# Decay matrices and v as float16 halves, v transposed by DMA, the state's fading on GpSimd, and a new order of steps on every engine

## What is computed

```python
z, x, B_proj, C_proj, dt_logits = split(u @ in_proj_w)
x = silu(causal_conv1d(x, conv_weight, conv_bias))        # 4 taps; gives v, 16 heads x 64
k, q = elu(B_proj) + 1, elu(C_proj) + 1                   # 64 states, shared by the heads
a = exp(-softplus(dt_logits + dt_bias) * exp(A_log))      # decay of each head and token
# inside a chunk: y_intra = ((q k^T) * exp(cs_s - cs_t), lower triangle) v
# between chunks: y_inter = exp(cs) q h_prev;  h = d * h + (k scaled)^T v
y = y_intra + y_inter + D_param * v
y = y * rsqrt(mean(y * y) + eps) * norm_scale * silu(z)
return y @ out_proj_w
```

## Time and profile before

| | |
|---|---|
| median of 3 runs | 1983.89 us (1983.5 to 1985.98) |
| profiled execution | 1986.14 us, its span 1984.4 us |
| mean granted TensorE clock | 0.973 of full speed |
| PE busy | 1877.7 us, 95% |
| DVE busy | 1470.5 us, 74% |
| ACT busy | 1019.4 us, 51% |
| POOL busy | 182.4 us, 9% |
| DMA | 107.37 MB, main queue 18.3% of 16 engines |

### The profile page before, as it was taken

One profiled execution on the slowest core, in us unless ns is written; L12 is line 12 of the kernel. 1 busy time (PEld: TensorE's weight loads), 2 busy tenths in 40 slices (PEclk: granted clock), 3 DMA queues, 4 the chain that ended last, 5 costly groups with the idle time before them and its releaser, 6 DMA issues.

```text
span 1984.4 us, 39342 instructions
## 1 busy us (share of the span) xinstructions
PE 1877.7 (95%) x13426; PEld 1337.4 (67%) x13426; DVE 1470.5 (74%) x3279; ACT 1019.4 (51%) x2247; POOL 182.4 (9%) x150
## 2 busy tenths in 40 slices
PE   5446899999999999999999999999999999999999
PEld 2123777767686767767676877777676867777675
DVE  6897686867677686867677686868677786867676
ACT  7836544536364554546363644546363645445363
POOL 0430010101000010101000010101000000101010
PEclk9668899999999999999999999999999999999999
DMA  8101112121212111121212111121212111121212
GB/s 321 68 19 35 28 44 64 37 54 53 54 43 49 47 43 48 37 54 53 54 46 49 43 45 46 37 58 49 53 54 43 53 40 40 40 67 37 53 54 53
DMA packets 147857, 107.37 MB, mean 54 GB/s; under 512 B 110030, under 2 KB 111158, under 8 KB 147254
## 3 DMA queue, kind: packets, MB, share of 16 engines
q1 hardware_dynamic: 147238, 105.51, 18.3%
q10 hardware_dynamic: 528, 1.05, 0.2%
HBM read 72.18 MB, written 8.65 MB: 41 GB/s over the span
## 4 chain that ended last, share of the span: by engine, by line
PE 92%; DVE 4%; ACT 1%; DVEq 1%; DMA 1%; issue 1%; SPq 0%; ACTq 0%; PEldq 0%
PE bank L827 88%; DVE wi L587 2%; PE bank L648 1%; PE bank L894 1%; PE bank L639 1%; DVEq L523 0%; DMA wi<-n_L_attn_out_proj_w_dram 0%; DVE wug L547 0%; DVE big L437 0%; PE bank L621 0%; DVE wd L437 0%; ACT wi L363 0%; DVE su_scale L526 0%; ACT wi L393 0%; ACT big L389 0%
## 5 line engine op out<-in xcount | busy, mean ns | idle before, releaser
L827 PE MATMUL bank<-xnT,wug 128*128 128x256 f16 x6144 | 705.1, 273 | 0.0
L827 PEld LDWEIGHTS bank<-xnT,wug 128*128 128x128 f16 x6144 | 600.6, 98 | 99.9
L827 PE MATMUL bank<-wd,h 128*128 128x512 f16 x1536 | 371.0, 379 | 0.0
L827 PEld LDWEIGHTS bank<-wd,h 128*128 128x128 f16 x1536 | 148.4, 100 | 157.2 <-issue 3.4
L1079 POOL TENSOR_TENSOR vw<-v,dec 128x512 f32<-128x512 f32 x64 | 73.9, 1155 | 1689.7 <-ACT v L1029 1239.7
L827 PE MATMUL bank<-wi,xnT 128*128 128x512 f16 (+1 forms) x1152 | 204.2, 330 | 16.4 <-DMA xnT<-cvx 16.4
L986 ACT ACTIVATE tg<-bank,gate_scale 128x256 f32<-128x256 f32 x256 | 119.7, 467 | 174.7 <-PE bank L827 139.1
L1035 ACT ACTIVATE Mx<-Mx,cs_own 128x128 f32<-128x128 f32 x512 | 162.1, 389 | 50.0 <-DMA Mx<-cs_rows 50.0
L1163 DVE SCALAR_TENSOR_TENSOR cvx<-xc,conv,cvx 128x256 f32<-128x256 f32 x384 | 169.0, 481 | 14.5
L827 PE MATMUL bank<-xnT,wi 128*128 128x256 f16 x1536 | 172.9, 273 | 0.0
L827 PEld LDWEIGHTS bank<-wi,xnT 128*128 128x128 f16 x1152 | 101.4, 99 | 104.6 <-issue 17.2
(11 more groups left out here) (241 smaller groups left out, 2386.5 us busy)
## 6 DMA issues: line engine op xcount, KB each, us to landing
Mx<-cs_rows SPq DMA_DIRECT2D x128, 256.0 KB, 3.5
cvx<-in_L_attn_u_dram SPq DMA_DIRECT2D x17, 512.0 KB, 3.4
Mx<-in_L_attn_u_dram SPq DMA_DIRECT2D x16, 512.0 KB, 3.7
out_dram<-Mx SPq DMA_DIRECT2D x16, 512.0 KB, 2.8
big<-in_L_ffn_W_down_dram SPq DMA_DIRECT2D x2, 2048.0 KB, 12.2
wug<-in_L_attn_in_proj_w_dram SPq DMA_DIRECT2D x2, 2048.0 KB, 12.8
pair<-in_L_ffn_W_gate_dram SPq DMA_DIRECT2D x4, 1024.0 KB, 5.3
pair<-in_L_ffn_W_up_dram SPq DMA_DIRECT2D x3, 1024.0 KB, 5.5
```

What stands on the lines that cost most here:

```text
L827: ins = nc.tensor.matmul(out, lhsT, rhs, start=first and n == 0, stop=last and n == len(pairs) - 1)
```

## The change

1. itr takes float16 halves. DVE's dec result M is followed by two new steps: mh (ACT copies M to float16, `M_hi`) and ml (DVE subtracts, `M_lo`). The halves lie in the bytes of M itself, or one q further. A scale C_M is folded into G, and itr's result is scaled back on DVE by S_ITR.
2. v is split into halves before it is turned: th on ACT (`v_hi`), tl on DVE (`v_lo`), and td on SP transposes both by DMA into the new array `v16`, tokens on partitions. The vt steps of PE and ACT go. itr is 8 heads x three products of float16, 64 columns each.
3. POOL first adds the two halves of v (into `vd`), then multiplies as before; its scales are folded elsewhere. y is written over v16 as float32.
4. sd: the state's multiplication by its decay goes from DVE to POOL, with a new semaphore `state_faded` for which DVE's st waits.
5. The copies of the halo go from DVE to ACT.
6. Some buffers move: y_hi and y_lo lie elsewhere, with new waits for the transposes that still read them; bd11 waits for itr01 in place of itr00.
7. All five lists of steps are reordered.

```diff
 PE_STEPS = """
-bc F0 xp0 xp1 xp2 F1 qk F2 cs D0 vt0 xp3 vt1 F3 F4 vt2 G D1 D2 F5 F6 int00 vt3 int01 D3 F7 D4 itr00 D5 F8 st00
-D6 F9 itr01 D7 F10 F11 z00 st01 int10 D8 itr10 D9 F12 z01 F13 int11 D10 itr11 st10 z10 F14 D11 z11 D12 F15 D13
-O0 D14 st11 D15 O1
+bc xp0 F0 xp1 qk cs F1 xp2 F2 F3 G xp3 D0 F4 F5 D1 int00 D2 F6 D3 int01 F7 F8 D4 itr00 F9 D5 F10 st00 itr01 D6
+F11 st01 int10 D7 z00 F12 D8 D9 F13 z01 D10 itr10 D11 int11 F14 itr11 z10 z11 F15 st10 D12 O0 D13 D14 st11 D15
+O1
 """.split()
 ACT_STEPS = """
-elu F0 xp0 xb0 xp1 xb1 xp2 sv0 qk F1 H0 F2 sv1 cs xb2 kh vt0 H1 H2 xp3 sv2 F3 vt1 xb3 H3 F4 vt2 dec00 dec01
-sv3 F5 H4 dec02 H5 F6 vt3 F7 dec03 vh00 H6 dec10 H7 F8 dec11 H8 F9 vh01 H9 sh00 ssq0 F10 dec12 z00 dec13 H10
-vh10 F11 sh01 z01 F12 H11 F13 yh00 ssq1 H12 xh0 yh01 H13 F14 sh10 vh11 xh1 z10 yh10 z11 H14 yh11 F15 H15 sh11
+elu xp0 F0 xb0 xp1 xb1 qk cs kh sv0 H0 F1 th0 sv1 H1 xp2 th1 F2 dec00 F3 H2 xb2 xp3 mh00 xb3 H3 F4 sv2 dec01
+sv3 th2 F5 H4 th3 dec02 F6 dec03 H5 H6 mh01 F7 F8 mh02 vh00 mh03 H7 H8 F9 F10 dec10 sh00 vh01 dec11 H9 dec12
+ssq0 H10 vh10 F11 dec13 F12 mh10 sh01 mh11 z00 H11 H12 mh12 yh00 z01 F13 mh13 yh01 ssq1 F14 z10 H13 yh10 z11
+vh11 H14 yh11 F15 xh0 xh1 H15 sh10 sh11
 """.split()
 DVE_STEPS = """
-fin bc F0 elu cv0 cv1 sv0 L0 F1 F2 sv1 qk cv2 L1 L2 sv2 F3 L3 F4 G cv3 dec00 dec01 sv3 kl F5 L4 L5 dec02 F6
-lna int00 F7 vl00 L6 itr00 lnb dec03 F8 L7 st00 F9 L8 int01 sl00 L9 itr01 dec10 dec11 vl01 F10 ssq0 int10
-dec12 st01 z00 L10 F11 vl10 sl01 itr10 z01 dec13 L11 int11 F12 itr11 lnc F13 yl00 L12 st10 yl01 ssq1 z10 L13
-F14 yl10 z11 xl0 yl11 L14 xl1 F15 vl11 L15 sl10 st11 sl11
+bc fin elu F0 cv0 cv1 sv0 F1 tl0 sv1 L0 qk tl1 L1 F2 G kl dec00 F3 L2 cv2 cv3 sv2 F4 L3 sv3 tl2 F5 tl3 L4
+dec01 dec02 F6 ml00 dec03 L5 L6 ml01 F7 F8 ml02 int00 itr00 vl00 ml03 L7 L8 lna st00 F9 F10 int01 vl01 sl00
+itr01 lnb int10 dec10 L9 dec11 vl10 L10 st01 F11 ssq0 ml10 dec12 F12 ml11 z00 sl01 L11 ml12 dec13 itr10 z01
+ml13 int11 yl00 itr11 F13 L12 yl01 ssq1 z10 F14 L13 yl10 z11 L14 lnc yl11 F15 xl0 xl1 vl11 L15 st10 st11 sl10
+sl11
 """.split()
 POOL_STEPS = """
-vw00 vw01 vw10 vw11
+sd00 vw00 vw01 sd01 vw10 sd10 vw11 sd11
 """.split()
 SP_STEPS = """
-store bw bd00 bd01 bd02 xin bd03 bd10 bd11 bd12 bd13 yd00 res yd01 yd10 yd11 xd
+store bw bd00 td0 td1 bd01 bd02 bd03 td2 td3 bd10 xin bd11 bd12 bd13 yd00 yd01 yd10 res yd11 xd
 """.split()
...
-                        if c == 1 and q % 2 == 0:
-                            sp.wait_ge(ring_filled, (i + 1) * NR + filled(f"itr0{q // 2}"))
+                        if c == 1 and q < 2:
+                            sp.wait_ge(ring_filled, (i + 1) * NR + filled(f"itr0{q}"))
...
+                    elif k == "td":
+                        n = at[0]
+                        if n == 0 and not first:
+                            for c in range(NT):
+                                sp.wait_ge(yT_loaded[c], i * 4 * 16)
+                                sp.sem_inc(turns, 1)
+                        sp.wait_ge(v_split, i * 4 + n + 1)
+                        sp.sem_inc(turns, 1)
+                        for u, src in enumerate((v_hi[n % 2], v_lo[n % 2])):
+                            sp.dma_start(v16[:, 2 * n:2 * n + 2, :, u, :].rearrange("p c t d -> p (c t) d"), src, transpose=True).then_inc(v_turned[n], 16)
...
-                        pe.wait_ge(act_emptied, (i + 1) * NR_ACT + emptied("vt3"))
+                        if c == 0 and hf == 0:
+                            for n in range(4):
+                                pe.wait_ge(v_turned[n], (i + 1) * 2 * 16)
                         o = bank(i, s)
                         for n in range(8):
-                            hd = 8 * hf + n
-                            ins = products(o[:, n * HD:(n + 1) * HD],
-                                           [(M[2 * hf + n // 4][:, n % 4, :], v[:, c, hd * HD:(hd + 1) * HD])])
+                            hd, q = 8 * hf + n, 2 * hf + n // 4
+                            ins = products(o[:, n * HD:(n + 1) * HD], three(lambda u: (M_hi, M_lo)[u][q][:, n % 4, :],
+                                                                           lambda u: v16[:, hd // 2, c, u, hd % 2 * HD:(hd % 2 + 1) * HD]))
...
+                    elif k == "th":
+                        n = at[0]
+                        act.wait_ge(vT_ready, (i + 1) * 4 + n + 1)
+                        if n == 0:
+                            act.wait_ge(ring_filled, i * NR + filled("st11"))
+                        if n >= 2:
+                            act.wait_ge(v_turned[n - 2], (i + 1) * 2 * 16)
+                        nc.scalar.activation(v_hi[n % 2], cv[n % 2].rearrange("p c t -> p (c t)"), ACT.Copy, scale=S_V).then_inc(v_high, 1)
...
+                    elif k == "mh":
+                        c, q = at
+                        if q == 0 and c == 0:
+                            act.wait_ge(ring_filled, (i + 1) * NR + filled("qk"))
+                            act.wait_ge(k_ready, i + 2)
+                        elif q == 0:
+                            act.wait_ge(ring_filled, (i + 1) * NR + filled("itr00"))
+                        else:
+                            act.wait_ge(M_ready, (i + 1) * 8 + 4 * c + q)
+                        act.wait_ge(M_whole, (i + 1) * 8 + 4 * c + q + 1)
+                        nc.scalar.activation(M_hi[q], M[q][:, :, :], ACT.Copy).then_inc(M_high, 1)
...
+                        pool.tensor_tensor(by_tile(vd[:, :]), v16[:, 4 * hf:4 * hf + 4, c, 0, :], v16[:, 4 * hf:4 * hf + 4, c, 1, :], ALU.add)
+                        pool.drain()
...
+                    elif k == "sd":
+                        c, hf = at
+                        n = 2 * c + hf
+                        pool.wait_ge(act_emptied, (i + 1) * NR_ACT + emptied("cs"))
+                        pool.wait_ge(state_ready, (i + 1) * 4 + n - 1)
+                        half = state[:, hf * 512:(hf + 1) * 512].rearrange("p (h d) -> p h d", d=HD)
+                        pool.tensor_tensor(half, half, bcast(dec3[:, 2, c, 8 * hf:8 * hf + 8], HD), ALU.mult).then_inc(state_faded, 1)
...
-                        nc.vector.tensor_copy(x[:, :, 0:TAPS - 1], halo[:, 2 * n:2 * n + 2, :])
...
-                                                ALU.mult).then_inc(M_ready, 1)
+                                                ALU.mult).then_inc(M_whole, 1)
+                    elif k == "ml":
+                        c, q = at
+                        dve.wait_ge(M_high, (i + 1) * 8 + 4 * c + q + 1)
+                        nc.vector.tensor_tensor(M_lo[q], M[q][:, :, :], M_hi[q], ALU.subtract).then_inc(M_ready, 1)
+                    elif k == "tl":
+                        n = at[0]
+                        dve.wait_ge(v_high, (i + 1) * 4 + n + 1)
+                        nc.vector.scalar_tensor_tensor(v_lo[n % 2], cv[n % 2].rearrange("p c t -> p (c t)"), S_V, v_hi[n % 2], ALU.mult, ALU.subtract).then_inc(v_split, 1)
...
-                        nc.vector.tensor_tensor(half.rearrange("p (h d) -> p h d", d=HD), half.rearrange("p (h d) -> p h d", d=HD),
-                                                bcast(dec3[:, 2, c, 8 * hf:8 * hf + 8], HD), ALU.mult)
-                        dve.drain()
+                        dve.wait_ge(state_faded, i * 4 + 2 * c + hf + 1)
```

More of the change, by code:

```diff
@@ L172, in program @@
         h_scale = sb("h_scale", [P, KF])
-        scal = sb("scal", [P, 10])
-        S_BC, S_DT, S_Z, S_Y, S_OUT, S_K, S_V, S_G, S_INT, S_Q = (scal[:, n:n + 1] for n in range(10))
+        scal = sb("scal", [P, 11])
+        S_BC, S_DT, S_Z, S_Y, S_OUT, S_K, S_V, S_G, S_INT, S_Q, S_ITR = (scal[:, n:n + 1] for n in range(11))
         WS_UG, WS_DP, SU_UG, SU_DP, NORM, CONVW, CONVB = 0, 32, 36, 40, 56, 64, 96
@@ L721, in program @@
         conv_done, vT_ready, M_exp, M_ready = sem("conv_done"), sem("vT_ready"), sem("M_exp"), sem("M_ready")
+        M_whole, M_high, v_high, v_split = sem("M_whole"), sem("M_high"), sem("v_high"), sem("v_split")
+        v_turned = [sem(f"v_turned{n}") for n in range(4)]
         cs_stored = sem("cs_stored")
@@ L965, in body @@
                         else:
-                            act.wait_ge(ring_filled, (i + 1) * NR + filled(f"vt{n - 2}"))
+                            act.wait_ge(v_turned[n - 2], (i + 1) * 2 * 16)
+                        nc.scalar.activation(halo[:, 2 * n:2 * n + 2, :], xc[n % 2][:, :, TB:TB + TAPS - 1], ACT.Copy)
                         for c in range(2):
@@ L1069, in _ @@
                         c, hf = at
-                        pool.wait_ge(act_emptied, (i + 1) * NR_ACT + emptied("vt3"))
+                        pool.wait_ge(act_emptied, (i + 1) * NR_ACT + emptied("cs"))
+                        if c == 0 and hf == 0:
+                            for q in range(4):
+                                pool.wait_ge(v_turned[q], (i + 1) * 2 * 16)
                         n = 2 * c + hf
```

87 lines of the change are left out of this document (47 added, 40 removed).

## The result

The changed kernel takes 1998.95 us in the median of four runs (1996.97 to 2000.48), the kernel before beside it 1984.54 us (1983.5 to 1985.98). The ratio is 1.0072, with a 95% interval of 1.0054 to 1.0089: slower by 14 us, where 78 us less were forecast. The profiled execution has a span of 1995.3 us.

What follows compares the result with a forecast made beforehand. PE, issuing without pause, was taken as the bound: 110.77 us a block less 5.32 gives 105.45, plus 0.45 of waits 105.9. 4.87 less over 16 blocks is -78 us, giving 1906 us, range 1888 to 1950.

Steps and rivals of the forecast that it cites:

- PE, removed and added: PE per block: itr's float32 products and vt leave, 8.68 us; 96 f16 pairs at 35 ns add 3.36; net -5.32 us.
- B: itr's small pair stays at about 57 ns, 1940 us, chance 0.12; at 81 ns, 1977 us, chance 0.02.
- rival D: itr's f16 pair load-bound at 108 ns (2018 us), or queue loss above 5.3 us a block; together chance 0.05.
- ACT and POOL: Busy per block: ACT net about +6.4 us to 62; POOL 8.6 us more, 17 in all.
- DVE: the sum: DVE per block: ml and tl added, fade and halo copies removed, net +4.2 us to 85.6 of 105.5, beside PE's work.
- The waits: PE waiting in four places of the new order: 0.45 us a block, each with about 0 to 3 us of cover.
- Rival C: DVE and ACT queues in fixed order make PE wait 2 to 4 us a block; 1947 us; chance 0.18.
- R2: Rival in the experiments: DMA transposes of v come late and cost the time; no chance given.
- (1): qk moves to behind three steps, 7.9 us after bc; kq ready at about +4.7 us, 3 us of cover.
- (2): G stands behind sv1, tl0, L0 and qk on DVE; a few tenths to 3 us ahead of PE.
- (3): Waiting on M_high puts DVE's and ACT's queues in lock step; F or L behind each ml; 0 to 3 us cover.
- (4): bd11 waits for itr01, so dec11 on ACT can be 1 to 2 us late, with H9 to F11 behind.

Runs made afterwards that it cites:

- the first experiment: Changed kernel with POOL's full-width vw and sd instructions replaced by fills that read nothing, waits kept: 1948.43 us, ratio 0.9817 to the kernel before.

## Why the prediction was wrong

**PE, removed and added: right.** The vt steps and the float32 products leave 8.7 us a block, and the small pair takes 29 ns, not 35: the low bound, the line through the 144- and 512-column pairs of the earlier trace rows. The direction of this choice was right and its allowance 0.6 us a block too large. Rivals B and D (57, 81 and 108 ns) fall. The Trainium skill's rule of 81 ns at 128 columns ("TensorE: Matmul & The Clock Gate", section on the back-to-back issue gap) would have made itr cost 7.8 us a block; the trace does not agree, here with 2.8. The same section's table, which gives up to 64 columns an issue floor of about 25 ns, is not contradicted: the measured 29 lies a little above it.

**ACT and POOL: right.** ACT 61.2 us where 62 was forecast, POOL 18.25 where 17 was. Neither holds PE.

**DVE: the sum was 3.8 us short.** Of its added and removed instructions the sum was right: with POOL's reads gone, DVE is busy for 84.7 us, where 85.6 was forecast. What was missing is 4.7 us of standing still beside POOL's reads. The step that failed stands under POOL: contention was seen in the groups, but it was priced on POOL's side alone, as a tenth of an instruction "on an engine that idles for 93 us of a block". The price on DVE's side was set at nothing. It needs no new evidence to see this: in the kernel before, one of DVE's tiny instructions (two numbers per partition) takes 169 ns at the least and 922 in the median, beside a POOL multiply (min/median/max ns):

```profile
L1115 DVE TENSOR_SCALAR rs<-mv x17: 169/922/996, 194.3 to 1918.1; 128x2 f32<-128x2 f32 x17
```

The Trainium skill's rule ("SBUF — State Buffer", section on who interferes with whom) was quoted and read for one engine only. The same section says that it is the order of issue that decides who is blocked, and that the blocked one stands fully. The trace agrees: DVE's 0.42 us become 1.38 when it starts behind POOL. It also says that an instruction with two inputs contends with one that reads and not with one that only writes, and the first experiment agrees, with L at 418 ns beside POOL's fills. The root's instruction with two numbers per partition has one input, and there the fills did hold DVE (569 ns).

**The waits: 6.6 to 7.0 us a block, forecast 0.45. This is the term that decided.** The period came out 5.8 us above the forecast of 105.9: 6.4 from the waits (7.0 less the 0.6 by which the forecast lay above PE's own work as it summed it, 0.45 and the 0.15 of the kernel before), less 0.6 from the pair. The step that failed is the sentence "This lies beside PE's work, as long as PE does not catch up with it", and in it the share of 81%, a mean over a block. I had looked for the cover in four places and taken each by its own chain; I had not read DVE's row by stretches. In the kernel before, the table of stretches of its second half shows it (the same columns as above):

```profile
363.13:373.13 10.00, 10.00 (x79) 7.71 (x78) 8.63 (x23) 6.24 (x17) 2.07 (x2) 1.00 0.19 53
373.13:383.13 10.00, 10.00 (x82) 7.90 (x80) 8.86 (x19) 5.64 (x14) 1.21 (x2) 1.00 0.15 52
383.13:393.13 10.00, 10.00 (x68) 6.75 (x67) 8.76 (x20) 4.29 (x10) 1.17 (x2) 1.00 0.00 0
...
413.13:423.13 10.00, 10.00 (x55) 5.18 (x53) 6.18 (x12) 1.56 (x4) 0.00 (x0) 1.00 0.40 79
423.13:433.13 10.00, 10.00 (x75) 6.31 (x74) 4.70 (x9) 0.91 (x2) 0.00 (x0) 1.00 0.27 80
```

Over 30 us behind itr00 DVE already stood at 86 to 89%, and in the changed kernel it holds PE at 87 to 92%: the rest of its time lies between its instructions. The share was a warning and not a proof, since at 89 to 94% in the first half it holds nobody. Of the 29 us that it idled in a block, 9 lay in the last two of these stretches. Of the eight ml that the change adds, six start in the stretch from 472.8 us on, in which DVE sets the pace, and PE's part of it became shorter at the same time. Rival C named this mechanism, with F behind ml and dec, and the profile shows its releasers; it was sized at 2 to 4 us, with a chance of 0.18, and "DVE idled 29 us a block without costing PE anything" was the argument that put it so low. What rival D adds at its end, a queue loss of more than 5.3 us, is what happened.

**How much belongs to what.** Taken away one at a time: POOL's reads 3.2 us a block, M_low's length 2.6, a part of the roots 2.2. The first two together give 3.9, so they overlap: each shortens the same row. These are shown. With M_low the length and the round trip are not told apart. That the order of the change has a share of its own is not shown: one other order was tried, and it left PE's waits for DVE as they were.

**SP and the transposes: right as far as seen.** No PE wait has v's transposes as releaser, so R2 falls. The 0.3 to 0.5 us at a block's start, for xnT, come from DVE's late end (its xl steps), with SP and the DMA behind.

**The places of the new order.** (1) and (2) had the cover they were given. (3) is where the waits came, at F11, F13, D11 and itr11, and it was given a few tenths. (4) cannot be told apart from (3).

**The condition** that the text gave, a period above 107.5 us, is met at 111.69.
